# Identity matmuls on TensorE in three waits and in the first attention, and the first pair of blocks taken up during the second gather

## The reference, cut to what matters

```python
x = x + _L0_attn_ref(_layernorm(x), ...)             # gated scan + feed-forward
x = x + _L0_xattn_ref(_layernorm(x), ctx, ctx, ...)  # attention 0: 16 heads of 8, rope, key mask
x = x + _L0_ffn_ref(_layernorm(x), ...)              # shared expert + top 2 of 8 routed experts
x = x + _L1_attn_ref(_layernorm(x), ...)             # attention 1: causal, only the top 24 queries of each head
x = x + _L1_xattn_ref(ctx, ctx, _layernorm(x), ...)  # attention 2: full mask
x = x + _L1_ffn_ref(_layernorm(x), ...)              # experts with capacity
```

## Time and profile before

| | us |
|---|---|
| median of 3 runs | 1094.67 |
| lowest and highest | 1091.3, 1103.55 |
| the profiled execution's own time | 1101.7 |
| its span, first to last instruction | 1100.0 |
| PE busy, PEld busy | 703.9, 451.0 |
| DVE, ACT, POOL busy | 481.0, 312.7, 240.3 |
| TensorE clock granted, mean over the span | 0.766 |

### The profile page before, as it was taken

One profiled execution on the slowest core, in us unless ns is written; L12 is line 12 of the kernel. 1 busy time (PEld: TensorE's weight loads), 2 busy tenths in 40 slices (PEclk: granted clock), 3 DMA queues, 4 the chain that ended last, 5 costly groups with the idle time before them and its releaser, 6 DMA issues. The chain is left out here.

```text
span 1100.0 us, 19023 instructions
## 1 busy us (share of the span) xinstructions
PE 703.9 (64%) x5168; PEld 451.0 (41%) x5169; DVE 481.0 (44%) x1183; ACT 312.7 (28%) x567; POOL 240.3 (22%) x370
## 2 busy tenths in 40 slices
PE   3434497547998686998044698854899844408860
PEld 2311233225776454655032466521566523305540
DVE  3454323453443442446343555443555343814431
ACT  1124422102445221443012144521244523003330
POOL 4442100040000123522621100013000021051225
PEclk9666698755656668999566799986699965759995
DMA  6589600085330002142148534106544010020002
GB/s 211 153 227 371 148 0 0 6 210 137 91 92 2 0 15 79 39 138 66 40 118 230 132 94 105 32 1 172 141 118 105 30 49 0 1 87 19 24 24 76
DMA packets 108233, 98.57 MB, mean 90 GB/s; under 512 B 9384, under 2 KB 99648, under 8 KB 103936
## 3 DMA queue, kind: packets, MB, share of 16 engines
q1 hardware_dynamic: 101952, 87.87, 29.8%
q0 software_dynamic: 3072, 6.30, 2.0%
q10 hardware_dynamic: 3152, 3.69, 1.0%
HBM read 53.53 MB, written 43.91 MB: 89 GB/s over the span
## 5 line engine op out<-in xcount | busy, mean ns | idle before, releaser
L1128 DVE TENSOR_REDUCE negm<-ps 128x4 f32<-128x512 f32 x192 | 124.6, 687 | 106.2 <-PE ps L1626 105.7
L810 ACT ACTIVATE wa<-ps 128x1024 f32<-128x1024 f32 x96 | 98.3, 1024 | 160.5 <-PE ps L1647 159.0
L1489 PE MATMUL ps<-ident,xn_tm 128*128 128x128 f32 x112 | 30.6, 427 | 149.0 <-DVE xn_tm L977 86.1
L1489 PEld LDWEIGHTS ps<-ident,xn_tm 128*128 128x128 f32 x112 | 19.8, 214 | 159.7 <-issue 143.6
L1626 PE MATMUL ps<-stack 75*128 75x128 bf16 x576 | 66.7, 258 | 10.2 <-DMA stack<-k_scr 8.9
L1663 PE MATMUL ps<-wa,f 128*32 128x128 f32 x1536 | 72.3, 314 | 1.5 <-ACT wa L810 1.0
L1647 PE MATMUL ps<-stack 75*128 75x128 bf16 x576 | 60.5, 244 | 8.3 <-DMA stack<-mT 8.3
L1626 PEld LDWEIGHTS ps<-stack 75*128 75x128 bf16 x576 | 51.3, 116 | 32.6 <-issue 18.1
L1647 PEld LDWEIGHTS ps<-stack 75*128 75x128 bf16 x576 | 49.5, 112 | 22.3 <-DMA stack<-mT 6.5
L1825 PE MATMUL ps<-w_gu,nT 128*128 x92 | 52.1, 649 | 3.2 <-issue 2.6
L552 POOL COPY f<-v0x 128x144 f32 x32 | 9.9, 309 | 195.4 <-ACTq L818 194.2
(11 more groups left out here) (330 smaller groups left out, 1476.3 us busy)
## 6 DMA issues: line engine op xcount, KB each, us to landing
k_scr<-parts SPq DMA_DIRECT2D x72, 192.0 KB, 2.8
q_scr<-parts SPq DMA_DIRECT2D x72, 192.0 KB, 2.9
stack<-q_scr SPq DMA_DIRECT2D x18, 600.0 KB, 5.5
stack<-k_scr SPq DMA_DIRECT2D x18, 600.0 KB, 7.5
w_w<-in_w SPq DMA_DIRECT2D x2, 2048.0 KB
wb<-q_scr SPq DMA_DIRECT2D x6, 600.0 KB, 5.6
f<-k_scr SPq DMA_DIRECT2D x6, 600.0 KB, 7.3
x_scr<-sel SPq DMA_DIRECT2D x2, 1472.0 KB, 9.1
```

Source lines behind the costliest of these rows:

```text
L810: link.release(act.activation(wa[:, u % 2, :], BF[u % 2], ACT.Exp, scale=SCALE), hWA.filled, hWA.at(stage, n * 4 + u), hB.freed)
L1128: v.tensor_reduce(negm[:, g4 * 4:g4 * 4 + 4, j], A[u % 2].rearrange("p (h k) -> p h k", h=4), AX.X, ALU.max, negate=True).then_inc(hA.free ...
L1489: last = tr(T[:, j * S:(j + 1) * S], src(j), ident[:, :])
```

## The change

Four things are changed. (1) TensorE gets `keep_warm(bank, count)`: matmuls of the bf16 identity with the identity repeated to 512 columns, whose result is overwritten. 16 of them stand ahead of the first scores of each of the three attentions, before the wait for the stack's load; one stands before each of the 64 units A of attention 0; 14 stand in each pair of `qp1` between the sum of |q| and the transpose of `sel`. (2) The wait for bank A's release is moved ahead of the wait for the stack, and the wait for bank T ahead of the wait for `sel`. (3) DVE takes the first pair of `qp1` between the statistics of blocks 0 and 1 and the second half's rows; `moe0_done` is said after the second half's statistics. POOL makes `rstd` of blocks 0 and 1 ahead of the second half's gathers, and that of blocks 2 and 3 after the first pair's key splits. (4) The slot numbers (`pos0_i`, `te0_i`) lie 16 columns further in the memory they share with `selT`, since `selT` of the first pair is now written while they are in use.

```diff
@@ POOL @@
             for h in range(2):
+                if h == 1:
+                    for n in range(2):
+                        block_stats("qp1", n)
                 g.wait_ge(slots_stored[h], 16 * PER)
...
-            stats("qp1")
-            split_stage("qp1", 2)
+            for i in range(NPAIR):
+                if i == 1:
+                    for n in range(2, NBLK):
+                        block_stats("qp1", n)
+                for p in range(2):
+                    split(g, chain, "qp1", 1, i * 2 + p, False)
@@ DVE @@
-            for n in range(NBLK):
-                if n >= 2:
+            for n in range(2):
+                statistics(n)
+
+            def second_half():
+
+                for n in range(2, NBLK):
                     for b in range(n * GB, (n + 1) * GB):
                         combine(b)
-                statistics(n)
-            v.sem_inc(moe0_done, 1)
-
-            query_stage(1)
+                    statistics(n)
+                v.sem_inc(moe0_done, 1)
+
+            for i in range(NPAIR):
+                query_pair(1, i)
+                if i == 0:
+                    second_half()
@@ PE @@
+            def keep_warm(bank, count):
+
+                for _ in range(count):
+                    mm(bank, identb[:, :], identb[:, :].unsqueeze(1).broadcast_to([128, 4, S]), start=True, stop=True)
...
                         last.then_inc(hU.filled, 1)
+                        pe.wait_ge(hT.freed, hT.at(stage, i * 4 + 2))
+                        keep_warm(T, 14)
                         pe.wait_ge(sel_ready, i + 1)
-                        pe.wait_ge(hT.freed, hT.at(stage, i * 4 + 2))
...
                     j, g4 = u // 4, u % 4
-                    if u == 0:
-
-                        pe.wait_ge(stack_loaded[s], m * LOAD + (len(range(s, NSTEP, 3)) * a + 1) * LOAD)
                     pe.wait_ge(hA.freed, hA.at(stage, n * 8 + u))
                     bank = A[u % 2]
+                    if isinstance(n, int) and n == 0 and u == 0:
+                        keep_warm(bank, 16)
+                    if u == 0:
+
+                        pe.wait_ge(stack_loaded[s], m * LOAD + (len(range(s, NSTEP, 3)) * a + 1) * LOAD)
+                    if a == 0:
+                        keep_warm(bank, 1)
```

More of the change, by code:

```diff
@@ L202, in program @@
         tot_g, tiles_g, end_g, start_g, base_g = (r0[:, k * 2 * E0:(k + 1) * 2 * E0] for k in range(5))
-        pos0, pos0_i = r0[:, 80:112], r0[:, 112:144].bitcast(i32)
-        te0, te0_i = r0[:, 144:144 + 2 * NT0], r0[:, 192:192 + 2 * NT0].bitcast(i32)
+        pos0, pos0_i = r0[:, 80:112], r0[:, 128:160].bitcast(i32)
+        te0, te0_i = r0[:, 160:160 + 2 * NT0], r0[:, 208:208 + 2 * NT0].bitcast(i32)
         tot0, cum0, excl0, off0 = (f[:, 2, k * S:(k + 1) * S] for k in range(4))
@@ L523, in _, with block_stats @@
             g.sem_inc(consts_ready, 1)
+            def block_stats(s, b):
+                g.wait_ge(stats_done, b + (STAT[s] + 1))
+                chain.settle()
+                link(g.tensor_tensor(ps_a[:, :], mv[:, bass.ts(b, GB), 1], eps_tile[:, :], ALU.add))
+                link(g.tensor_tensor(rstd[:, bass.ts(b, GB)], ps_a[:, :], halves[:, 0, 0:GB], ALU.pow))
+                g.sem_inc(rstd_done, 1)
             def stats(s):
                 with chain.loop(NBLK, 2) as b:
[L528 to L532, removed]
+                    block_stats(s, b)
             def split_stage(stage, per, rope=False):
@@ L1086, in query_stage, with query_pair @@
             def query_stage(a):
-                stage = "qp%d" % a
                 with link.loop(NPAIR, (4, 2 * 3 + SELECT_LINKS, 3)[a]) as i:
+                    query_pair(a, i)
+            def query_pair(a, i):
+                    stage = "qp%d" % a
                     for p in range(2):
@@ L1612, in scores @@
                     j, g4 = u // 4, u % 4
+                    pe.wait_ge(hA.freed, hA.at(stage, n * 8 + u))
+                    bank = A[u % 2]
+                    if isinstance(n, int) and n == 0 and u == 0:
+                        keep_warm(bank, 16)
                     if u == 0:
                         pe.wait_ge(stack_loaded[s], m * LOAD + (len(range(s, NSTEP, 3)) * a + 1) * LOAD)
-                    pe.wait_ge(hA.freed, hA.at(stage, n * 8 + u))
-                    bank = A[u % 2]
+                    if a == 0:
+                        keep_warm(bank, 1)
                     if a == 1:
```

## The result

The changed kernel takes 1085.81 us (median of 4 runs, 1080.54 to 1088.03). The kernel before, run on the same chips, takes 1097.41 (median of 4, 1091.3 to 1103.55). The ratio is 0.9891 with a 95% interval of 0.9849 to 0.9933: faster by 11.6 us, between 7 and 17, and so just over the 1% that the forecast asked for, with an interval on both sides of it. The forecast was 1078, 16.7 less than before. The forecast had drawn its line for "faster" at 1083.7, 1% under the 1094.67 that it knew; 1085.81 lies above that line, and passes the 1% only because the kernel before came out at 1097.41 with a fourth run. The profiled execution took 1086.43 us, close to its median; that of before, 1101.7, was above its own.

A forecast was written before the change was run, and what follows sets the result against it. Bounds: TensorE at half clock in attention 0, and one chain, no single engine, between routed experts and attention 1. Terms -8 + 0 + 5.1 + 0 - 11.4 - 2.4 = -16.7 us, from 1094.7 to 1078; range 1066 to 1100, own range 1070 to 1086.

The forecast's parts named there:

- Attention 0, -8: One identity before each unit A raises the clock, warm share 0.85, 11.9 us a warm step: -8 us, all warm -12.6.
- rival 3: More than forecast: attention 0 all warm with its identities hidden, -16 us there, 1070 in all; chance 0.1.
- The rule that a busy engine is released: The skill's clock rule: attention 0, always busy, would already be at full clock, so more matmuls only add length.
- rival 1: Attention 0 stays at half clock and pays for its identities: +22 in place of -8, 1108 us; chance 0.13.
- the mixed case: Attention 0 at a warm share of 0.35 to 0.7, between +9 and -2 there, about 1090 us; chance 0.17.
- 16 before attention 0 and 2: 0: The 16 identities ahead of attentions 0 and 2 fit PE's waits for the stack: 0 (to +1.6 for attention 0).
- 16 before attention 1, +5.1: The 16 identities there lie on the path, 6.1 us, first maxima about 1.0 us sooner: +5.1 us.
- The first pair during the second gather, -11.4: Between routed experts and attention 1, the second pair's normalising comes at 568.5 instead of 579.91: -11.4 us.
- the queue, -2.4: Stack loads start further ahead of the second pair's stores, shortening DVE's 7.09 us wait for the query parts' store: -2.4 us.
- Contention, 0: DVE's normalising and splits beside the gathers slow them by 1.6 us at most, taken as 0.
- Rival 2: The reordering brings nothing, gathers slowed by DVE or the early select costing what it saves: 1092 us; chance 0.15.

The follow-up runs named there:

- e2: The changed kernel with the new order but no identity matmuls at all (the three keep_warm calls gone); 1088.74 us, ratio 0.9914 against the kernel before.
- e6: The changed kernel with two identities before each unit A of attention 0, 16 a step; 1085.92 us.
- second execution of before: The kernel before, unchanged, profiled once more after the result; that execution took 1096.53 us.
- e8: The changed kernel with 6 more identities in each attention's last step's wait and 2 before each further unit B of attention 0's last step; 1075.37 us.
- e10: The changed kernel with early key split, identities in last steps' waits, none of the 16 before attention 1, one identity before every other unit A; 1069.69 us.
- e1: The changed kernel with every identity kept but the old order of the second half and qp1; 1097.37 us, ratio 0.9994 against the kernel before.
- e4: The changed kernel without the one identity before each unit A of attention 0, the 16 ahead kept; 1085.73 us.
- e7: The changed kernel with POOL's key split of block 0 after the fifth of the second half's 16 gathers; 1078.21 us, ratio 0.9842 against the kernel before.

## Why the prediction was right, and where it was off

The verdict, faster by over 1%, came as forecast, at its lower edge, and 1085.81 lies in the range of 1066 to 1100 and, by 0.2 us, within the forecast's own 1070 to 1086. The gain was over by 5 us. Point by point:

- **Attention 0, -8: right in the total, by luck, and not in its make-up.** Every step from the second on was at the full clock (share 1.00, not 0.85), and a warm step took 11.2 to 12.0 and mostly 11.2 us, not 11.9: the identities cost next to nothing visible. Steps 2 to 7 sum to 68.1 us for 81.5 in the execution that the forecast was made on (not the 84 of six times 14.0: the last took 11.4), -13.4, beyond the bound of -12.6 and inside the -16 of rival 3, whose mechanism this is. But that execution was the coldest of three (the others 78.8 and 75.6), so against their mean it is -10.5. Then the tail took 2.0 us more than before's mean, and the start nets +0.9. That is -7.6, the table's -7.5: a step that gained more than forecast, a baseline that was colder than most, and a tail that was not in the sum cancel.
- **The rule that a busy engine is released** had the time of rival 1 as its consequence. Here the engine that was busy 64.72 of 69 us had a clock of 0.57, and with identities, busy 49.89 of 57 us, 1.00. The Trainium skill, "TensorE: Matmul & The Clock Gate", part 1, is not borne out for this mix of matmuls: by these rows being busy is not enough. Neither rival 1 nor the mixed case beside it happened in any of nine kernels with identities in the steps' units.
- **16 before attention 0 and 2: 0, right.** In attention 0 the scores came 1.8 us late, and the first step is 15.2 us for 17.4. In attention 2 the first maxima come 50.4 us after the end of attention 1 for a mean of 53.7 before, but the second ones 69.3 us for 70.0: what the first step starts sooner it waits longer.
- **16 before attention 1, +5.1: right in sign, a little large.** They take 6.2 us as worked out; taken out, they gave some 3.5 us in the stretch's traces and 4.4 by the medians. They don't pay, as the term said.
- **The first pair during the second gather, -11.4, and the queue, -2.4: right in kind, a little large.** The key split took 4.06 us (533.50 to 537.56; forecast 4.1), the sum 2.07, `qn` to the end of `sel` 4.2 (3.9), from its first row to the normalising 10.5 (10.0; the first row took 1.25 us for 0.35). The 14 identities took 3.91 us (4.8) and were done before `sel`. DVE's wait for the query parts is 4.91 us for 7.09. From the end of attention 0 to the second pair's last normalising: 209.2 us, for 219.1 as the mean of the three before, -9.9. From there to the first maxima the two kernels without the 16 take 34.8 us, the three before 36.9: -2.1. The excess here and that of the 16 cancel: for the whole stretch the terms sum to -8.7, and the table has -8.6. e2, the reordering without the 16, has -10.8 for a forecast of -13.8.
- **Contention, 0: right.** The slowest gather took 1.10 us, beside DVE's split, for 0.94; sixteen took 20.1 us. The forecast's reading of the 1.05 us in the earlier trace rows was loose: the gather just before it had the same kind of DVE work beside it and took 0.95.
- **What failed is the zero that was never written down**: that attention 1, attention 2 and the rest stay as they were. They took 486.7 us for a mean of 481.2 before, 5.5 more, and that is nearly the whole of the miss. In attention 1 and 2 the tails make 2.4 and 2.2 of it. A tail has two parts, and each grew.
  - *The last stored maxima land later.* PE goes on 2.71 us after DVE's last copy begins in all nine tails of before, and after 3.97, 2.71 and 4.50 us in the changed kernel's three, though SP issues the stores as soon after the copy as before. That is 1.3 of the 2.0 us in attention 0, nothing in attention 1 and 1.8 of the 2.2 in attention 2. Such late landings stand in 18 of the 27 tails of the kernels with identities in attention 0's steps, and in 1 of the 15 of the others. So they go with the identities, though not always (e6 has none in three); by what way, no run shows.
  - *The clock falls behind the wait,* and the last matmuls run partly at half of it. PE at the last maxima of attention 1, before and in the changed kernel, then windows of each behind it:

```profile
710.92 0.39 PE L1639 MATMUL ps<-identb,causal 128*128 128x512 bf16 x1 [1.41 <-DMA stack<-mT]
...
689.55 0.61 PE L1672 MATMUL ps<-identb,causal 128*128 128x512 bf16 x1 [1.42 <-DMA stack<-mT]
```

```profile
713.00:719.00 6.00, 5.01 (x79) 3.25 (x77) 1.05 (x5) 3.98 (x6) 0.00 (x0) 1.00 0.01 3
691.00:697.00 6.00, 6.00 (x62) 4.10 (x59) 0.72 (x3) 2.71 (x4) 0.00 (x0) 0.59 0.00 0
```

  The wait is the same and the clock is not: 0.99 from there to attention 1's end before, 0.79 in the changed kernel, and 0.87 in the second execution of before, whose tail is 16.2. In the 36 tails of the kernels that leave this wait empty, the clock from there to the attention's end was 0.97 or more behind 8 of 22 waits of 0.8 to 1.4 us and never above 0.88 behind the 14 of 2.3 to 3.2 us. So the later landing makes the fall likelier, and part of the fall differs by execution; how much of the 2.4 us in attention 1 is the change's, **isn't shown**. With the wait filled (e8, e10) it was 0.93 or more in all six tails.
- **Rival 2, that the reordering brings nothing**, is refuted by e2 (0.9914, upper end 0.9957). Rather the other half of the change is the one that brings about nothing as it stands (e1: 0.9994): attention 0's gain (2.8 us in e1's trace) is eaten in the next stretch (+5.1), where the 16 before attention 1 lie. All that the runs show to save time in the change as it stands is the reordering.

Open: by what way identities in attention 0 go with late landings of the last maxima, why e2's trace shows 10.8 us in its stretch and its median 7.7 in all, and what sets the clock of attention 0 in a given execution of before. The last two are of the size by which executions of one kernel differ (1091.3 to 1103.55).

## What to carry to other kernels

Before pricing a stage by one profile, look whether its clock is a property of the kernel or of that execution: the same 69 us read 0.57, 0.65 and 0.75. Identity matmuls belong where the engine would otherwise idle, in the waits of a last step above all, and only as many as hold the clock (four a step did what eight and sixteen did); put on the path ahead of work that warms itself up, 6.2 us of them cost about 3.5. And look at the whole time: a stage whose steps got shorter by identities (e4 against the changed kernel) left the median where it was. When a stage is moved up behind a long row of DMA issues, ask which small operation that another engine waits for stands behind them in the same queue: moving it forward was worth 4.1 us in the traces of that stretch and 7.6 by the medians.

## What the runs showed of the hardware

- **Being busy was not enough for TensorE's clock.** Attention 0's mix (75-row bf16 scores, 32-column f32 products, transposes) kept PE busy 94% of 69 us at a mean clock of 0.57; four full 128x512 bf16 matmuls by the identity in each step made it 0.99.
- **A wait of 1.4 us was followed by either clock, waits of 2.3 to 3.2 us never by the full one throughout.** In attention 0's last step, after 2.67 us of waiting, 13 us at 0.52 and a tail of 17.3 us; after six identities and a remaining wait of 1.27 us, 1.00 and 15.0 us. In attention 1, 0.99 after 1.41 us before and 0.79 after 1.42 us in the changed kernel.
- **The landing of a small store varied by 0.8 to 1.8 us with nothing changed at its issue.** SP issued the second store of the last maxima 0.79 us after DVE's copy began in all 42 tails; PE went on 2.7 us after that copy began in 23 of them, and 3.55 to 4.5 us in the other 19.
- **POOL's key split held up DVE by more than DVE's split held up the gathers.** DVE's weighted sum of a row, 0.35 us alone, took 1.25 us beside POOL's key split in the changed kernel (546.26 to 547.51, POOL's last operation of the split 546.21 to 547.36) and 1.29 in e7, while a gather's issue beside DVE's split went only from 0.94 to 1.10. The Trainium skill, "SBUF — State Buffer", section "SBUF: two separate sides", has the pair of ports that the two share as an exclusive lock, which also a DVE operation with two inputs from SBUF takes against a POOL operation that reads SBUF; the rows of 1.25 and 1.29 us agree.
